# One transfer per step on SP's queue, ahead of the gathering reads, and the context norms one step later

## The reference

```python
x = x + _L0_xattn_ref(_layernorm(x), ctx_1024, w_kv, w_q, w_out1, w_out2, gamma)     # 16 heads of 64
...
x = x + _L1_xattn_ref(ctx_1024, _layernorm(x), mask_BxS2_bk1, Wq, Wkv, Wo, ...)      # 8 heads of 64
```

## Time and profile before

| | us |
|---|---|
| median of 3 runs | 2745.32 (2742.64 to 2751.34) |
| the profiled execution | 2746.7 |
| its span, first to last instruction | 2745.0 |
| PE busy | 2365.8 (86%) |
| DVE busy | 1801.5 (66%) |
| ACT busy | 1272.3 (46%) |
| POOL busy | 730.0 (27%) |

### The profile page before, as it was taken

One profiled execution on the slowest core, in us unless ns is written; L12 is line 12 of the kernel. 1 busy time (PEld: TensorE's weight loads), 2 busy tenths in 40 slices (PEclk: granted clock), 3 DMA queues, 4 the chain that ended last, 5 costly groups with the idle time before them and its releaser, 6 DMA issues. The chain is left out here.

```text
span 2745.0 us, 62358 instructions
## 1 busy us (share of the span) xinstructions
PE 2365.8 (86%) x23416; PEld 1905.2 (69%) x23416; DVE 1801.5 (66%) x4001; ACT 1272.3 (46%) x2509; POOL 730.0 (27%) x907
## 2 busy tenths in 40 slices
PE   8998999999999899977868888887877378999986
PEld 6876787777877778866756666766743237888873
DVE  7779677777777777766866656656643347666625
ACT  5544454454544445434634444544411334555553
POOL 1434043431434324330134444445100000001000
PEclk9999999999999999987979989988977669999996
DMA  7766776777777777765637777877757654444310
GB/s 261 207 204 205 218 212 198 211 229 224 220 203 209 220 217 217 206 192 205 217 121 225 234 221 234 243 223 229 215 200 313 251 184 153 124 135 136 94 51 23
DMA packets 187238, 541.02 MB, mean 197 GB/s; under 512 B 26076, under 2 KB 121520, under 8 KB 180800
## 3 DMA queue, kind: packets, MB, share of 16 engines
q1 hardware_dynamic: 184416, 528.55, 62.4%
q0 software_dynamic: 2304, 8.39, 0.9%
q10 hardware_dynamic: 224, 0.10, 0.0%
HBM read 356.76 MB, written 180.19 MB: 196 GB/s over the span
## 5 line engine op out<-in xcount | busy, mean ns | idle before, releaser
L497 PE MATMUL l0x_psum<-l0x_fast 128*128 128x512 f32 x1764 | 439.4, 401 | 1.3 <-DVE l0x_fast L699 0.8
L497 PEld LDWEIGHTS l0x_psum<-l0x_fast 128*128 128x128 f32 x1764 | 325.7, 190 | 92.5 <-issue 24.3
L611 ACT ACTIVATE l0x_sbuf<-l0x_sbuf 128x896 f32<-128x896 f32 x224 | 234.5, 1047 | 250.8 <-DVE l0x_sbuf L722 250.8
L1794 DVE CUSTOM_DVE_ANT_0 l3x_sbuf<-l3x_psum,key_bias,l3x_sbuf 128x896 f32<-128x896 f32 x224 | 249.1, 1150 | 92.7 <-PE l3x_psum L1638 76.8
L1724 ACT ACTIVATE l3x_sbuf<-l3x_psum 128x512 f32<-128x512 f32 x392 | 221.4, 599 | 179.0 <-PE l3x_psum L1656 172.4
L477 PE MATMUL l0x_psum<-l0x_fast 128*128 128x448 f32 x1344 | 299.8, 372 | 0.3 <-DVE l0x_fast L684 0.3
L538 PE MATMUL l0x_psum<-l0x_sbuf 128*32 128x128 f32 x6272 | 219.4, 294 | 80.3 <-DMA l0x_sbuf<-turns 65.3
L538 PEld LDWEIGHTS l0x_psum<-l0x_sbuf 128*32 128x32 f32 x6272 | 184.5, 116 | 118.1 <-DMA l0x_sbuf<-turns 70.8
L477 PEld LDWEIGHTS l0x_psum<-l0x_fast 128*128 128x128 f32 x1344 | 244.2, 188 | 26.1 <-issue 0.4
L722 DVE CUSTOM_DVE_ANT_0 l0x_sbuf<-l0x_psum,l0x_sbuf 128x896 f32<-128x896 f32 x224 | 248.9, 1149 | 20.1 <-PE l0x_psum L512 19.9
L742 DVE STREAM_TRANSPOSE l0x_sbuf<-l0x_sbuf 128x896 f32<-128x896 f32 x224 | 236.9, 1096 | 0.6 <-issue 0.6
(11 more groups left out here) (778 smaller groups left out, 4425.6 us busy)
## 6 DMA issues: line engine op xcount, KB each, us to landing
turns<-l0x_sbuf SPq DMA_DIRECT2D x112, 896.0 KB, 5.0
l0x_sbuf<-turns SPq DMA_DIRECT2D x448, 224.0 KB, 4.3
turns<-l1x_sbuf SPq DMA_DIRECT2D x56, 896.0 KB, 6.6
l1x_sbuf<-turns SPq DMA_DIRECT2D x224, 224.0 KB, 4.2
last_keys<-ctx_high SPq DMA_DIRECT2D x112, 224.0 KB, 3.5
ahead<-in_L_ffn_W SPq DMA_DIRECT2D x18, 1024.0 KB, 13.3
experts<-in_L_ffn_W SPq DMA_DIRECT2D x18, 1024.0 KB, 12.7
l0x_sbuf<-in_ctxT SPq DMA_DIRECT2D x14, 896.0 KB, 8.0
```

The lines of the kernel that those rows point to most:

```text
L497: mm = pe.matmul(ps[:, :], x[:, c, t * T:(t + 1) * T], weights[w][:, c, :], start=(j == 0), stop=(j == len(products) - 1))
L611: act.activation(p, p, ACT.Exp, scale=-1.0, bias=self.negm[:, n % 2, 2 * pr + a:2 * pr + a + 1], accum_out=self.rs[:, m % self.RING, a:a + ...
L1794: dve.tensor_tensor_reduce(junk[:, a, :].rearrange("p (i c) -> p i c", i=2), ps_s[a][:, :, 0:HALF], bias[:, n * CH:(n + 1) * CH].bitcast(F ...
```

## The change

In SP's program the transfers of a chunk no longer stand together behind the gather of pr = 1. A new function `chunk_transfer` issues at most one of them per step, between the step's scatter and its gather: at pr = 0 the rows (l0x) or the means and rstds (l1x), at pr = 1 the load of the chunk (after the wait for c_low), at pr = 2 the mask (l1x, after the wait for the bias) or the first store (l0x), at pr = 3 the second store. At the end of l0x the output weights are issued after the last gather. On POOL `pool_norm` moves from pr = 1 to pr = 2.

```diff
         for m in range(self.P * NCH):
             n, pr = divmod(m, self.P)
             self.sp_scatter(sp, m)
+            self.chunk_transfer(sp, n, pr)
+            self.sp_gather(sp, m)
+            if m == 0 and self.side is None:
+                self.sp_out(sp)
             if m == self.P * NCH - 1 and self.side is not None:
                 sp.wait_ge(self.s.sem("sum_ps"), NCH)
                 self.sp_out(sp)
-            self.sp_gather(sp, m)
-            if m == 0 and self.side is None:
-                self.sp_out(sp)
-            if self.side is not None and pr == 0 and n > 0:
-                self.side.sp_rows(sp, n)
-            if pr == 1 and n + 1 < NCH and (n + 2 < NCH or self.parts_dram is not None):
-                self.sp_loads(sp, n + 2)
+
+    def chunk_transfer(self, eng, n, pr):
+
+        s, ahead = self.s, n + 2
+        if pr == 0 and n > 0 and self.side is not None:
+            self.side.sp_rows(eng, n)
+        if pr == 0 and ahead < NCH and self.norm_dram is not None:
+            for c in range(DC):
+                eng.wait_ge(s.sem(f"scaled{c}"), ahead)
+            self.sp_norm(eng, ahead)
+        if pr == 1 and ahead < NCH:
+            eng.wait_ge(s.sem("c_low"), 2 * ahead)
+            self.sp_raw(eng, ahead)
+        if pr == 2 and ahead < NCH and self.mask_dram is not None:
+            eng.wait_ge(s.sem("bias"), ahead)
+            self.sp_mask(eng, ahead)
+        if pr in (2, 3) and ahead <= NCH and self.parts_dram is not None:
+            self.sp_save(eng, n + 1, pr - 2)
...
-    def sp_save(self, sp, n):
+    def sp_save(self, sp, n, part):
         s = self.s
         sp.wait_ge(s.sem("c_low"), 2 * n + 2)
-        for part in range(2):
-            sp.dma_start(self.parts_dram[part].rearrange("(c p) k -> p c k", c=DC)[:, :, n * CH:(n + 1) * CH],
-                         self.ctx[part][:, n % 2, :, :].bitcast(F32)).then_inc(s.sem(f"saved{n % 2}"), 16)
+        sp.dma_start(self.parts_dram[part].rearrange("(c p) k -> p c k", c=DC)[:, :, n * CH:(n + 1) * CH],
+                     self.ctx[part][:, n % 2, :, :].bitcast(F32)).then_inc(s.sem(f"saved{n % 2}"), 16)
...
-            if pr == 1 and self.norm_dram is not None and n + 2 < NCH:
+            if pr == 2 and self.norm_dram is not None and n + 2 < NCH:
                 self.pool_norm(pool, n + 2)
```

More of the change, by code:

```diff
@@ L416, in sp_loads @@
         if self.parts_dram is not None:
-            self.sp_save(sp, n - 1)
+            for part in range(2):
+                self.sp_save(sp, n - 1, part)
     def sp_mask(self, sp, n):
```

## The result

The changed kernel takes 2673.84 us (2671.05 to 2678.37), beside 2744.57 us (2742.64 to 2751.34) for the kernel before on the same chip: a ratio of 0.974 [0.9718, 0.9761]. The profiled execution spans 2676.7 us (before 2745.0), at a mean granted clock of 0.929 (before 0.915). The gain is 71 us, where 106 were forecast (the prediction's sum is 107, and 2638 stands in it as 2639). Lines have moved: the scatter is L409, the gather L417, the load L439, the stores L451, PE's values L553, its turn of their result L561, ACT's context copy L597 and its copy of the values L633, POOL's last norm L827 and c_low L837.

What follows compares the result with a forecast made beforehand. Bound: PE's wait for turned probabilities, held up by three bulk transfers on SP's queue. Gains of 71 (l0x), 2 (tail) and 34 (l1x), 107 us, from 2745.3 gave 2638, rounded to 2639; forecast band 2615 to 2670 (56%), range 2587 to 2700.

Steps and rivals of the forecast that it cites:

- the second rival: Rival, 18%: c_low ahead of the gather takes the burst's place; gain 27 + 2 + 6, 2710 us.
- from c_low to the landed gather: At pr 1: load lands about 4.2 us after c_low, gather 4.3 later, 8.5 us in sum.
- The time that c_low leaves: At pr 1, from c_low's end until PE wants the values: 8.41 us in l0x, 6.18 in l1x.
- the whole stall: In l0x: 55.2 us of waits in 13 plus 19 for slow steps, in sum 74 us.
- Tail: End of l0x: last gather ahead of the output weights, issue to values 8.92 to 6.84 us, gaining 2 us.
- gather of pr 1 late behind c_low and load: l1x, pr 1: the 8.5 us chain against 6.18 us available, late by 2.3 us per chunk.
- norms late, ACT's copies later: l1x: norms one step later on POOL delay ACT's copies and thus c_low, about 1.6 us per chunk.
- slow step at the lower clock: l1x: a slow step of PE following the late gather, 1.7 us per chunk.
- The wait moves: The second rival, 18%: gather costs 5.1 us, l0x keeps 3.6 us loss per chunk, l1x nearly all; 2710 us.
- The whole gain: Rival, 17%: context copy in time, short waits do not slow PE's clock; l0x 74, l1x 12 x 6.2, tail; 2595 us.
- Slower: Rival, 5%: a transfer holds a gather over 2.55 us, l0x late at pr 1 to pr 3; about 2818 us.

Runs made afterwards that it cites:

- e6_l0x_load_pr4: The changed kernel with l0x's load of the raw chunk at step 4 instead of step 1, l1x unchanged; 2649.60 us.
- e1_norms_pr1: The changed kernel with POOL's norms back at pr 1, SP's order as changed; 2658.15 us.
- e3_context_first: The changed kernel with POOL making the next context's low half at the head of pr 0, before waiting for alpha; 2609.57 us.
- e10_both_load_behind: e4_both with the load of the raw chunk at step 1 behind that step's gather instead of in front; 2628.74 us.
- e4_both: The changed kernel with the edits of e1_norms_pr1 and e3_context_first together; 2600.42 us.
- e7_all_behind: e4_both with every transfer of the chunk issued behind the gather instead of in front; 2737.19 us.

## Why the prediction was right, and where it was off

The time, 2674 us, lies in the range (2587 to 2700) and on the forecast's side; the forecast's own number is 35 us too low, and its own band ended at 2670: the range holds the time because it takes in most of the second rival. The waits moved where they were told to move; one price was too small, the cost of the late norms fell in another place than told, and some of the signs it names did not come.

**The price that failed: from c_low to the landed gather.** The prediction put 4.2 us on the load, from a lone scatter's 3.71 and two additions for which it names no row, and 4.3 on the gather behind it, 8.5 in sum. The profile's list of DMAs gives the load's median from issue to landing in the changed kernel (transfer, count, KB, us):

```profile
l0x_sbuf<-in_ctxT SPq DMA_DIRECT2D x14, 896.0 KB, 5.6
...
soon<-in_ctxT SPq DMA_DIRECT2D x14, 896.0 KB, 5.5
```

A load lands 5.5 us after its issue, 1.3 more than assumed; the gather's landing follows it by 3.6 to 4.4 us in 23 of the 24 chunks of both stages in which it stands right behind, near the assumed 4.3. Most of that could have been read before the change. In the trace of the kernel before one load, at 1401.87 us, goes out after 5 us (1395 to 1400) with a DMA share of 0.00, and takes 5.1 us, not a scatter's 3.7 (list of DMAs of 1400 to 1410 us, same columns):

```profile
soon<-in_ctxT SPq DMA_DIRECT2D x1, 896.0 KB, 5.1
```

From c_low to the values it is 9.67 us in the l0x chunk above and 9.33 in the l1x chunk (means of ten chunks 9.62 and 9.77), where the forecast had 8.5. The time that c_low leaves was right: 394.19 less 1.18 less 384.52 is 8.49 us (forecast 8.41) and 1588.91 less 3.14 less 1579.58 is 6.19 (6.18). What is left over is the load. The Trainium skill, "DMA: Bandwidth & Descriptors", section "Queues, rings and completion order", has each engine take its descriptors in ring order, and the trace now agrees for a gather behind a load, by these 3.6 to 4.4 us. The estimate of 2.1 us for the bytes by the Trainium skill, same page, section "Anatomy of one DMA" (a fit for another issue path), points the other way than the miss.

**l0x, 54 us instead of 71** (56.5 less 2.2 of the tail). Forecast were 0.1 us lost at pr 1 and 0.1 at pr 2. Measured are, over twelve chunks, 0.9 to 1.4 at pr 1 (mean 1.16) and 0.15 to 1.2 at pr 2 (mean 0.67); the mean chunk is 1.74 us above the 79.07 of the kernels without a wait, where 0.2 was forecast. The second of these was mis-sized, too: scatter, store and gather were to take 8.8 us from the values of pr 1 to those of pr 2, and take 9.4. The waits of the twelve chunks are 22 us, where under 10 were told for all steps but the last two, and e6_l0x_load_pr4, which moves only the load there, to a step where c_low is long done, gets 24 back. The estimate of the whole stall, 74 us, is near: 54 and 24 are 78. That the chunk would come to "near 79" was wrong by these two terms.

**Tail, 2 us.** 6.68 us from gather to values, forecast 6.84: right.

**l1x, 13.8 us instead of 34.** The terms of a chunk, measured as means over ten chunks of the changed kernel's trace: the wait of the values of pr 1, and the steps that end at the values of pr 0 (10.36 us) and of pr 2 (10.60), each less the 8.57 that they take without a wait:

| lost per chunk | forecast | measured |
|---|---|---|
| gather of pr 1 late behind c_low and load | 2.3 | 3.6 |
| norms late, ACT's copies later | 1.6 | 1.8 |
| slow step at the lower clock | 1.7 | 2.0 |
| sum | 5.6 | 7.4 (40.84 less 33.63 is 7.2) |

The gather's term is the load's price again: 2.3 and 1.1 are 3.4. That the norms would make ACT 2 us late was right (2.25), and so was their cost, but not the place: I added it to the gather's wait, as if only c_low moved. PE pays it already at the turn of pr 0, where it waits 1.33 us for ACT's copy of the values, and then wants its gather as much later as c_low comes. e1_norms_pr1 shows it: without the late norms the turn's wait is gone and the gather's is the same. The slow step is dearer where the lower clock lasts 6.8 instead of 3.4 us. The 1.6 us between 5.6 and 7.2 are, in 12 chunks, 19 of the 20 us missing.

**What came as told, and what did not.** The stall of l0x's pr 2 and its slow steps went; ACT idles before its second context copy; transfers between scatter and gather cost l0x nothing when their semaphore is early (e6_l0x_load_pr4, and e3_context_first); a bulk transfer in the queue's path is 2.5 us (e10_both_load_behind: 2.50); the l1x wait moved from pr 2 to pr 1. Its size did not come as told: 3.1 to 4.4 us for 2 to 4, and the chunk is 40.84 us for 38 to 40. And PE waits for POOL's context before a value group for only 0.7 us, in two waits.

**The rivals.** "The wait moves" described what happened, more than the forecast did, and its 2710 went too far because no slow steps came in l0x. "The whole gain" needed the context in time: with that, in e4_both, the kernel takes 2600 us, 5 more than that rival's 2595. One reason given for it was misread: waits under 2.04 us do not stand at the ends of stages only, l0x has 1.14 and 0.94 us at pr 2 of its third and thirteenth chunk in the kernel before. "Slower" asked that a transfer hold a gather longer than its 2.55 us, by order or by shared engines; ahead of the gather it does not, but e7_all_behind shows how close it lies: the same transfers on the other side of the gather cost 137 us.

## What to carry to other kernels

On this in-order queue, which carries a write and a dependent read in each step, the bulk load was better placed between the two than behind the read where its semaphore was done in time (2600 us against 2629); with the late semaphore it was better behind the read (2628 against 2674). Price such a step from the late semaphore to the last landing, with the load's own issue-to-landing time, and advance the producer of the semaphore (here one move on POOL, worth 64 us) before moving the transfers. Compare the write and the read by themselves with the step they must fit in, before what stands between them. A move that costs nothing beside a stall must be priced again when the same change removes that stall.

## What was not expected of the hardware

- A load of 896 KB in front of a gather lands 5.5 to 5.6 us after its issue (medians of 14), where a lone scatter of the same size was 3.71 us from issue to the gather; a load that met idle engines took 5.1.
- Waits of 0.9 to 1.4 us at pr 1 of l0x of the changed kernel and of 0.2 to 2.7 us in the stretch shown of e4_both left the granted clock at 1.00, while at a wait of 2.14 us further on in the same kernel (values at 1722.05) it fell to 0.50 for 3.4 us; in l1x of the changed kernel, where PE waits 3.1 to 4.4 us, each such wait has a stretch of 3.4 or 6.8 us at 0.50 around or right behind it.
- Moving the same transfers behind the gather lowers the DMA share from 0.89 to 0.76 and lengthens the kernel by 5%: with a dependent pair on the queue, the engines' share says little on what is left to gain.
